# Moving the q/k stores and the copies of the row maxima from SyncE's queue to ScalarE's

## What is computed

```python
x = x + 0.5 * ffn0(layernorm(x))      # gate/up/down, operands rounded to FP4 in blocks of 16
x = x + mamba(layernorm(x))           # projection, short convolution, selective scan over 512 steps
x = x + 0.5 * ffn0(layernorm(x))
x = x + 0.5 * lora(layernorm(x))      # base linear layer and 8 gated rank-8 experts
x = x + attention(layernorm(x))       # 16 heads of 16, causal, ALiBi bias, softmax
x = x + 0.5 * lora(layernorm(x))
```

## Time and profile before

| | |
|---|---|
| median of 3 runs | 5165.4 us (5162.62 to 5176.22) |
| profiled execution, its own time | 5150.52 us |
| its span in the profile | 5148.7 us |
| PE busy | 4193.1 us, 81% |
| DVE busy | 4050.5 us, 79% |
| ACT busy | 2378.0 us, 46% |
| POOL busy | 1569.2 us, 30% |
| DMA moved | 753.44 MB, 146 GB/s |

### The profile page before, as it was taken

How to read it: one execution, slowest core, us unless ns; L and a number is a source line. 1 busy time by engine, 2 the same in 40 slices (tenths; PEclk the granted TensorE clock), 3 DMA queues, 4 the chain that set the end, 5 groups by cost and what they waited for, 6 DMA issues and landing times.

```text
span 5148.7 us, 54829 instructions
## 1 busy us (share of the span) xinstructions
PE 4193.1 (81%) x18639; PEld 2082.1 (40%) x18669; DVE 4050.5 (79%) x5964; ACT 2378.0 (46%) x4341; POOL 1569.2 (30%) x1036
## 2 busy tenths in 40 slices
PE   3455788888888888888888888888888888887777
PEld 2122434444343444444343444434354444434343
DVE  5486878889788988978787888978798898877522
ACT  1333454544545454554545454454545445454322
POOL 0142424323242423324142332324242332414100
PEclk9677899999999999999999999999999999998887
DMA  1475766767676766768566676766666676767400
GB/s 54 122 173 137 160 161 147 157 148 169 159 169 157 159 160 142 173 150 179 145 157 159 151 159 151 169 158 162 151 158 158 145 174 158 169 150 163 89 19 29
DMA packets 241436, 753.44 MB, mean 146 GB/s; under 512 B 37650, under 2 KB 132659, under 8 KB 171524
## 3 DMA queue, kind: packets, MB, share of 16 engines
q1 hardware_dynamic: 241156, 749.95, 63.0%
HBM read 647.30 MB, written 101.71 MB: 145 GB/s over the span
## 4 chain that ended last, share of the span: by engine, by line
DVE 34%; PE 33%; ACT 10%; issue 9%; DMA 6%; POOL 5%; SPq 2%; another core or an unknown queue 0%; DVEq 0%; ACTq 0%; POOLq 0%
DVE state L1450 8%; DVE u L1445 6%; PE m L978 5%; DVE mt L1538 4%; POOL state L599 4%; DMA state<-dtx_scratch 4%; PE m L950 4%; PE m L990 3%; PE pd L1175 2%; PE y L1042 2%; ACT shared L839 2%; DVE front L1272 2%; SPq L454 2%; DVE front L1387 2%; DVE front L1274 1%
## 5 line engine op out<-in xcount | busy, mean ns | idle before, releaser
L599 POOL TENSOR_TENSOR state<-state,bc 128x1024 f32<-128x1024 f32 x512 | 1205.3, 2355 | 2048.0 <-DVE u L1445 2048.0
L1450 DVE TENSOR_TENSOR_SCAN state<-decay,u 128x1024 f32<-128x1024 f32 x512 | 1168.4, 2282 | 31.2 <-ACT decay L769 21.4
L950 PE MATMUL m<-w_gu,hats_m 128*128 128x480 f32 (+1 forms) x1536 | 698.2, 596 | 78.0 <-DVE front L1363 73.2
L769 ACT ACTIVATE decay<-decay,a_neg 128x511 f32<-128x511 f32 x1024 | 683.1, 714 | 54.5 <-DMA decay<-dt_scratch 54.3
L1445 DVE TENSOR_TENSOR u<-state,bc 128x1024 f32<-128x1024 f32 x512 | 649.6, 1269 | 40.6 <-DMA state<-dtx_scratch 36.3
L978 PE MATMUL m<-w_dn,front 128*128 128x256 f32 (+1 forms) x1536 | 431.8, 427 | 71.3 <-ACT front L705 71.3
L950 PEld LDWEIGHTS m<-w_gu,hats_m 128*128 128x128 f32 x1536 | 291.0, 200 | 423.2 <-issue 253.5
L1042 PE MATMUL y<-state,sel 128*32 128x512 f32 x2048 | 292.7, 645 | 203.3 <-POOL state L599 203.1
L978 PEld LDWEIGHTS m<-w_dn,front 128*128 128x128 f32 (+1 forms) x1536 | 300.4, 208 | 193.1 <-ACT front L705 103.1
L686 ACT ACTIVATE front<-m 128x240 f32<-128x240 f32 (+1 forms) x384 | 139.5, 364 | 395.7 <-PE m L950 377.1
L990 PE MATMUL m<-hats_m,w_in 128*128 128x512 f32 x512 | 287.2, 692 | 33.9 <-DVE front L1404 16.5
(11 more groups left out here) (258 smaller groups left out, 7270.0 us busy)
## 6 DMA issues: line engine op xcount, KB each, us to landing
decay<-dt_scratch SPq DMA_DIRECT2D x256, 1024.0 KB, 7.3
state<-dtx_scratch SPq DMA_DIRECT2D x256, 1024.0 KB, 11.4
qk_scratch<-shared SPq DMA_DIRECT2D x64, 384.0 KB, 3.0
shared<-qk_scratch SPq DMA_DIRECT2D x384, 64.0 KB
kh<-qk_scratch SPq DMA_DIRECT2D x384, 64.0 KB
xs_scratch<-front SPq DMA_DIRECT2D x16, 1024.0 KB, 6.1
dt_scratch<-front SPq DMA_DIRECT2D x256, 64.0 KB, 1.9
dtx_scratch<-hats_m SPq DMA_DIRECT2D x256, 64.0 KB, 1.7
```

The lines of the kernel that those rows point to most:

```text
L599: eng.tensor_tensor(st, st, bc[:, 1:2, :].to_broadcast([P, WIDE, L]), ALU.mult).then_inc(scan_pool.sem, scan_pool.step(f"c{r}{h}"))
L769: ins = eng.activation(d, d, ACT.Exp, scale=a_neg[:, g:g + 1])
L950: mm = eng.matmul(f.bank(f"gu{t}{p}")[:, 0:2 * width], f.norm.hat_t[:, k, t * P:(t + 1) * P], w_gu[:, k, 2 * lo:2 * (lo + width)], start=( ...
L1450: eng.tensor_tensor_scan(st, decay[:, n % ND, h * WIDE * L:(h + 1) * WIDE * L], u[:, :], 0.0, ALU.mult, ALU.add).then_inc(scan_dve.sem, sc ...
```

## The change

The four stores of the q/k parts and the three copies of the rows of maxima leave SP's program and stand in ACT's, right behind the operation that makes their data. ACT waits there for its own operation to finish, then issues the DMA. Two waits are new: ACT's first exponential of a pass waits for all stores of the pass, as its output lies over `qk_parts`; and PE's first score waits for the last third part. The due times of SP's stores fall away with them; the loads stay where they are.

```diff
@@ SP
             def attention(r, q):
-                for n in range(4):
-                    yield 13.2 + 2 * n
-                    eng.wait_ge(att_act.sem, att_act.after(r, f"three{n}"))
-                    eng.dma_start(qk_scratch[n].rearrange("w p l -> p w l"), qk_parts[:, n % 2, :, :]).then_inc(qk_saved[n // 2], 16)
-
...
-                def load_maxima(j):
-                    eng.wait_ge(att_act.sem, att_act.after(r, f"m{j}"))
-                    for w in range(3):
-                        eng.dma_start(qh[MAXROW + w:MAXROW + w + 1, j % 2, :, :], m_rows[w * G:(w + 1) * G, :]).then_inc(m_loaded, 16)
-
                 yield 20
                 load_set(0)
                 load_set(1)
                 for k in range(NG):
                     w, j, t = kind(k - 1)
                     yield GROUP_AT(k) + 2.15
-                    if w == "s" and t == T - 1:
-                        load_maxima(j)
                     if w == "e" and t == T - 1 and j < 2:
                         load_set(j + 2)
@@ ACT
                         eng.activation(qk_parts[:, n % 2, w, :], (PG, PU)[n % 2][:, :], ACT.Identity, bias=bias_qk[:, n % 2, n // 2:n // 2 + 1]
                                        ).then_inc(att_act.sem, att_act.step(f"{name}{n}"))
+                    eng.wait_ge(att_act.sem, att_act.after(r, f"three{n}"))
+                    eng.dma_start(qk_scratch[n].rearrange("w p l -> p w l"), qk_parts[:, n % 2, :, :]).then_inc(qk_saved[n // 2], 16)
...
                     eng.activation(m_rows[:, :], att_bank[f"m{j}"][0:3 * G, :], ACT.Copy).then_inc(att_act.sem, att_act.step(f"m{j}"))
+                    eng.wait_ge(att_act.sem, att_act.after(r, f"m{j}"))
+                    for w in range(3):
+                        eng.dma_start(qh[MAXROW + w:MAXROW + w + 1, j % 2, :, :], m_rows[w * G:(w + 1) * G, :]).then_inc(m_loaded, 16)
...
                         yield GROUP_AT(k) + 0.5 * g + 0.3
+                        if j == 0 and t == 0 and g == 0:
+                            for saved in qk_saved:
+                                eng.wait_ge(saved, 32 * (r + 1))
                         eng.wait_ge(att_pe.sem, att_pe.after(r, f"e{j}{t}{g}"))
@@ PE
                         if w == "s":
+                            if j == 0:
+                                eng.wait_ge(att_act.sem, att_act.after(r, "three3"))
                             eng.wait_ge(qk_loaded[b], SET_LOADS * (2 * r + j // 2 + 1))
```

## The result

The changed kernel takes 5361.1 us in the median of 4 runs (5346.68 to 5364.08); the kernel before, run beside it, 5165.86 us (5162.62 to 5176.22). The ratio is 1.0386, 95% interval 1.037 to 1.0402: slower by 195 us, where +67 us was forecast and 5285 us was the top of the range. The profiled execution took 5359.63 us, with a span of 5357.8.

What follows compares the result with a forecast made beforehand. No single engine was taken as the bound, but a path hopping between in-order engines. 57.5 + 5 + 8 - 2 - 5.1 + 3.7 = +67 us, 5232 us on the median of the runs; range 5160 to 5285.

Steps and rivals of the forecast that it cites:

- the landing of the second store: ACT's wait for store 1: landing 0.35 us longer a pass beside SP's earlier loads, 5 us; bounds 0 and +3.8 a pass.
- the sum: All terms added against the profiled execution: 57.5 + 5 + 8 - 2 - 5.1 + 3.7 = +67 us.
- rival A: Not slower: an issue takes under 0.1 us on ACT, so SP's freeing remains, 5155 us; chance 0.13.
- the holds: ACT held by issuing copies of the maxima, 3.83 us a pass, 57.5 us over fifteen passes, +3.7 in the last.
- m1 and m3: Copies of these two rows of maxima delay the operations queued behind them on ACT: 1.75 and 1.93 us a pass.
- m0 and m2: Copies of the other two rows of maxima on ACT: 0.15 us a pass and nothing, mostly covered.
- The clock: TensorE's clock falling behind ACT's holds: 0.5 us a pass, 8 us; bounds nothing or 60 us in all.
- SP freed, last pass: PE's 5.12 us wait for the first set's loads in the last pass goes: -5.1 us.
- the 2 us of scan loads: SP's scan loads go 1 to 17 us earlier, ending two waits, 2 us together.
- B: Worse: store landings at the long end (+30 us) or a clock that falls behind each hold (+30), 5290 us; chance 0.11.
- C: Absorbed: ACT's holds are real but half of them vanish into later idle time, 5195 us; chance 0.18.

Runs made afterwards that it cites:

- run 1: Kernel after with the copies of the maxima back on SP, so only the four stores are on ACT: 5302.35 us, ratio 1.0271.
- run 4: Kernel before with the second store due behind the pair of scan loads on SP's own queue, nothing on ACT: 5310.6 us, ratio 1.0284.
- run 12: Kernel before with the second store on SP moved between the decay load and the state load: 5227.37 us, ratio 1.0125.
- run 8: Kernel before with only the copies of m1 and m3 on ACT, plus the change's two new waits: 5230.02 us, ratio 1.0141.
- run 2: Kernel after with the four stores back on SP at their old due times, only the maxima on ACT: 5229.51 us, ratio 1.0128.
- run 9: Kernel after with the maxima on SP, stores on ACT, SP waiting for stores 0 and 1 to land before the loads: 5159.45 us, ratio 0.9999.

## Why the prediction was wrong

**The step that failed** is the landing of the second store: "I take 0.35, near the median, since before too the loads followed after 0.5 us: 15 x 0.35 = 5 us", with "bounds 0 and +3.8 a pass". It measured +9 us in the pass shown (12.01 against 3.05), of which ACT waits 10.33 - 1.95 = 8.4. On PE, where it counts, L1106's wait grew from 9.1 us in all (L1110 before, 5 times) to 134.5: +125 us. The stores alone cost +140 us in run 1, against 5 - 2 - 5.1 = -2 us in the sum.

Two readings went into this. First, the working had both numbers, the load "at 2694.03 instead of 2695.11" and the store at 2694.62, and so the change of sides, 0.49 us behind to 0.59 us ahead. It took them for the same overlap. Runs 4 and 12 show that the side decides and not the overlap: behind one load 7.5 us, behind both 11.3 to 12, ahead of both 3. Second, the bound of +3.8 a pass came from the longest landing of before, 6.8 us, taken as a landing beside loads. Looked at one by one, the stores of 5.4 to 6.8 us in the trace of before are the fifteen third ones. Each of them left 5.8 to 6.6 us behind the state load, on the same queue, and landed 0.8 to 2.2 us behind that load. The one of the pass in the earlier trace rows, with its landing:

```profile
2702.25 0.37 SPq L513 DMA_DIRECT2D qk_scratch<-shared  x1
...
DMA to landing us min/median/max: 5.7/5.7/5.7
```

It landed at 2707.95, 0.8 us behind the state load (2695.67 + 11.48 = 2707.15). So the trace of before already held stores behind 2 MB: the 6.8 us were what was left of the loads' landing, and a store that leaves right behind them has all of it ahead. The landing of the loads in that stretch was 7.4 and 11.5 us. With that as the bound, 8.5 a pass, the range would have reached past 5300 us.

The Trainium skill, "DMA: Bandwidth & Descriptors", section "Queues, rings and completion order", says that an engine takes turns between the queues it has work for, a packet at a time. The trace agrees for the second half of the store's time: 81 packets of q1 and 80 of q10 in 3 us. It doesn't for the first half: while the 128 packets of the decay load start, none of q10's does, in the 5.4 us after the store left. Nor do the turns make the store early here, as a packet of the load carries eight times the bytes. By landing, the queue changes little: 12.01 us on ACT's queue (the kernel after), with 9.4 us of ACT's wait a pass (151.2 / 16, run 1), against 11.3 us and 10.4 us (166.9 / 16) on SP's own queue, where the store left 0.6 us later (run 4). The same page's "Issuing engines are not separate DMA queues", which the prediction cited for its rival A, says that DMAs from different engines run on the same 16 engines and interleave. The 81 and 80 packets agree with this; nothing is won by the second queue.

**Right in mechanism, near in size: the holds.** 1.94 us at L835 against 1.75 and 1.93 forecast for m1 and m3, an issue of 580 ns against 573. The maxima alone cost +66 us; the sum gave 57.5 + 3.7 and a part of the 8 for the clock. That m1 and m3 carry it is run 8, where they cost +73 us (interval 64 to 81) against the 59 that the sum gave for them. m0 and m2 were put at 2 us and measured some 8 (interval 3 to 14), so they were slightly too cheap.

**The clock, too small in the sum.** Stretches of 4 us from the hold at 1016 on in the kernel after, and at the corresponding place of the pass of the earlier trace rows in the kernel before (busy us of PE, PEld, DVE, ACT and POOL; granted clock; DMA share; GB/s):

```profile
1016.00:1020.00 4.00, 2.05 (x11) 0.60 (x14) 3.87 (x3) 1.75 (x5) 2.34 (x1) 0.50 0.01 3
1020.00:1024.00 4.00, 4.00 (x22) 0.89 (x14) 0.00 (x0) 1.85 (x4) 0.00 (x1) 0.53 0.00 0
...
2760.00:2764.00 4.00, 4.00 (x27) 1.87 (x23) 0.45 (x1) 2.98 (x6) 0.56 (x1) 0.83 0.98 231
```

The second one follows 4 us in which PE was busy for 2.05 and is still near 0.50, that is 1.2 GHz, where 0.83 was granted before. It is not one pass alone. Over the first fifteen passes, the clock granted 4 to 8 us behind the copy to `m_rows` is 0.90 in the mean before and 0.57 with the maxima on ACT (run 2) for m1, and 0.99 and 0.62 for m3. In the kernel after it is 0.51 in the stretch 8 to 16 us behind the second store, where it was 1.00 before. The time at 1.2 GHz is 946 us in all before, 1094 in run 2, 1065 in run 1 and 1216 in the kernel after.

The forecast took 0.5 us a pass, "as two such rows do not say that the clock will fall again"; it does fall behind most holds. What that costs can only be accounted for, as no run separates it. With the maxima alone (run 2) the profiled spans differ by 79.5 us. PE's wait behind the exponential grew by 50 (61.8 against 12.0), its busy time by 45 (4238.1 against 4193.1), and its other waits shrank by 15. By this account some 30 us of the 79.5 are slower matmuls, not 8, and the wait is less than the 61 of the forecast's holds; that the two add up to about the measured +66 would then be partly luck. For the whole change PE's two waits grew by 125 and 50 and its busy time by some 60 us, missing records left out, which is 26 more than the 209 us; its other waits must have shrunk by that.

**SP freed, last pass.** The 5.12 us wait is gone from the trace, as forecast. Its gain, with the 2 us of scan loads, is below what run 9 can tell.

**The rivals.** A (a short issue) is out by the 580 ns. B had both of the right things: "store landings at the long end", at a quarter of its size (+2 us a pass where it is over 8), and "a clock that falls behind each hold" (+30, about what the account above gives). Its argument against late landings, "the landings of before overlapped them too", was the same mistake as the forecast's. C, half absorbed: the holds weren't absorbed, since PE waits for 62.3 us behind them and run 2 lost 66.

**What stays open.** Why no packet of the store on ACT's queue moves until those of the decay load on SP's have started isn't shown. That it lands with the state load fits the turns of 1 KB against 8 KB, but a store of larger packets wasn't tried, nor one of fewer. How the loss parts between waits and clock wasn't separated.

## What to carry to other kernels

When a wait is taken out of an in-order queue, list what stood behind it, and ask not only whether it will come sooner, but past which transfers it will now go; a wait that looks like loss, here 478.6 us on SP, can be what keeps a short transfer that someone waits for ahead of long ones that nobody does. Bound the landing of an overtaken transfer by the landing of those that overtake it, not by its own history. And when a row gives a minimum and a maximum, look at which transfers made the maximum: here they were those that already stood behind the loads. Ask, too, of a landing on the chain how long its cover lasts: here it was full to within 0.1 us, so that making it shorter gave nothing that could be measured and making it longer cost nearly all.

## What the runs showed of the hardware that was not expected

- A 384 KB store that left 0.03 us behind the second of two 1 MB loads landed after 12.01 us, 0.1 us behind that load (944.35 + 11.9); between the loads 7.5 us (run 12, one queue); ahead of both 3.05 us. Behind both it took about as long on SP's queue as on ACT's (11.3 and 12.01 us).
- On a queue of its own, the store between the loads took 11.5 us: it took turns with the later load packet for packet (81 and 80 in 3 us), 1 KB against 8 KB. In the pass shown first it started no packet in the 5.4 us in which the earlier load's packets started.
- ACT issues a copy of the maxima in 580 ns in the median (SP: 573) and a store in 366 ns (SP: 366): here the price of an issue goes with the DMA's shape more than with the engine. It isn't fixed either: a store that SP issued right behind a load held it for 560 to 590 ns (runs 12 and 4).
- PE near 1.2 GHz (0.57 granted in the mean of fifteen passes) from 4 to 8 us behind the copy to `m_rows` when a hold of 1.8 us follows it, as above.
